# Retrieval scores on one core: one resident chunk fewer, one chunk pair more, biases seeded into PSUM by ScalarE

## What is computed

```python
retrieved = jnp.mean(item_embeddings[indices], axis=1)          # [512, 512]
fused_input = jnp.concatenate([user_rep, retrieved], axis=1)    # [512, 1024]
fused_rep = fused_input @ W_fuse + b_fuse                       # [512, 512]
logits = fused_rep @ W_proj + b_proj                            # [512, 12500]
```

## Time and profile before

| | us |
|---|---|
| runs | 309.22, 310.26, 312.52 |
| median | 310.26 |
| the profiled execution | 309.87 |
| its span, first to last instruction | 308.0 |
| PE busy | 296.9 |
| VectorE busy | 248.3 |
| ScalarE busy | 128.1 |
| POOL busy | 74.9 |

### The profile page before, as it was taken

The page is one execution under the profiler, slowest core; times in us unless marked ns, Lnnn a source line. Parts: engine busy times, 40 slices in busy tenths (PEclk is TensorE's granted clock), DMA queues, the critical chain, the costliest instruction groups (busy, mean ns, idle before and its releaser), DMA issues.

```text
span 308.0 us, 4024 instructions
## 1 busy us (share of the span) xinstructions
PE 296.9 (96%) x1384; PEld 242.3 (79%) x1384; DVE 248.3 (81%) x371; ACT 128.1 (42%) x164; POOL 74.9 (24%) x76
## 2 busy tenths in 40 slices
PE   3999999699999999999999999999999999999995
PEld 1559887498888889888887888888888888888884
DVE  5898998778987836999689989979799797996123
ACT  1104664430010012435375575655846458463310
POOL 4766886787777200000000000000000000000000
PEclk9999999999999999999999999999999999999999
DMA  7999999999996322367538966839677494343315
GB/s 271 337 377 312 358 400 377 409 361 403 291 304 211 107 100 69 130 226 277 198 137 324 318 257 220 313 136 292 240 239 295 146 360 159 135 138 128 131 70 199
DMA packets 32547, 75.13 MB, mean 244 GB/s; under 512 B 4511, under 2 KB 20655, under 8 KB 32528
## 3 DMA queue, kind: packets, MB, share of 16 engines
q1 hardware_dynamic: 25264, 58.06, 52.6%
q0 software_dynamic: 5536, 13.73, 13.6%
q10 hardware_dynamic: 1728, 3.10, 2.6%
HBM read 52.85 MB, written 25.60 MB: 255 GB/s over the span
## 4 chain that ended last, share of the span: by engine, by line
PE 80%; DMA 10%; DVE 6%; issue 1%; ACT 1%; POOL 0%; SPq 0%; POOLq 0%; DVEq 0%; ACTq 0%
PE pair L1137 25%; PE pair L1215 15%; PE pair L1217 15%; PE pair L1218 15%; DMA early<-w_proj 7%; PE pair L1083 4%; PE pair L1123 3%; DMA ring<-item_embeddings,rows 2%; DVE w_lo L833 2%; DVE w_lo L919 1%; DMA early<-w_fuse 1%; DVE pair L796 1%; PE pair L1168 0%; DVE t_sums L908 0%; PE pair L1089 0%
## 5 line engine op out<-in xcount | busy, mean ns | idle before, releaser
L440 POOL DMA_INDIRECT ring<-item_embeddings,rows x56 | 59.8, 1067 | 20.3 <-issue 14.0
L1137 PE MATMUL pair<-w_hi,f_hi 128*128 128x500 f32 x144 | 56.7, 394 | 1.8 <-DVE w_lo L833 1.8
L1137 PE MATMUL pair<-w_lo,f_hi 128*128 128x500 f32 x144 | 56.3, 391 | 0.0
L1137 PE MATMUL pair<-w_hi,f_lo 128*128 128x500 f32 x144 | 56.0, 389 | 0.0
L1215 PE MATMUL pair<-w_hi,s_hi 128*128 128x500 f32 x128 | 49.9, 390 | 0.0
L1217 PE MATMUL pair<-w_lo,s_hi 128*128 128x500 f32 x128 | 49.9, 390 | 0.0
L1218 PE MATMUL pair<-w_hi,s_lo 128*128 128x500 f32 x128 | 49.8, 389 | 0.0
L796 DVE SCALAR_TENSOR_TENSOR pair<-ring,mask,pair 128x512 f32<-128x512 f32 x48 | 36.1, 752 | 3.3 <-DVE pair L810 0.5
L1215 PE MATMUL pair<-w_hi,f_hi 128*128 128x500 f32 x96 | 37.3, 389 | 0.1
L1218 PE MATMUL pair<-w_hi,f_lo 128*128 128x500 f32 x96 | 37.2, 388 | 0.0
L1217 PE MATMUL pair<-w_lo,f_hi 128*128 128x500 f32 x96 | 37.2, 387 | 0.0
(11 more groups left out here) (138 smaller groups left out, 433.2 us busy)
## 6 DMA issues: line engine op xcount, KB each, us to landing
w_raw<-w_proj SPq DMA_DIRECT2D x26, 500.0 KB, 8.1
early<-w_proj SPq DMA_DIRECT2D x24, 500.0 KB, 6.7
logits<-part_out SPq DMA_DIRECT2D x21, 500.0 KB, 3.4
logits<-out_sb SPq DMA_DIRECT2D x28, 250.0 KB, 2.3
logits<-out_sb SPq DMA_DIRECT2D x10, 500.0 KB, 3.0
logits<-out_sb ACTq DMA_DIRECT2D x8, 250.0 KB, 7.0
early<-b_proj SPq DMA_DIRECT2D x8, 250.0 KB, 9.9
s_sum<-b_proj SPq DMA_DIRECT2D x8, 250.0 KB, 6.9
```

Source lines behind the costliest of these rows:

```text
L440: return nc.gpsimd.indirect_dma_start(out=to, out_offset=None, in_=table, in_offset=bass.IndirectOffsetOnAxis(ap=column, axis=0), **how)
L1137: m = nc.tensor.matmul(ps[:, 0:CHUNK], f[:, t, k, :], w, start=begin, stop=(f is f_lo and k == HK - 1))
```

## The change

- `RESIDENT` goes from 8 to 7, `ROUNDS` from 8 to 9. The single chunk 8 and its banks, loads and evacuations are gone.
- ScalarE handles the groups of blocks 1 and 2 and the first three of block 3 (`COPIED = 24` groups with block 0): `seed(t, c)` copies a bias row from SBUF into the bank before PE's first matmul there, the 12 matmuls add onto it, and `copy_out` copies the bank into the output slot. PE waits for `seeded` instead of for an evacuation. Only groups (3, 3) to (3, 6) are still evacuated with an addition by VectorE; their bias rows come in one DMA into `part_out`.
- The bias rows 0 to 3 are loaded after chunk 6 has landed, into the half of `early` that chunk 3 has left, and rows 4 to 6 when chunk 6 is split.
- The list product of tile 1 (`turn_slots`) moves from ahead of the block's last chunk into its middle, next to the turn. VectorE adds tile 1's slots 8 to 10 before it makes `w_lo` of chunk 6's second half, and the home row in the middle of chunk 5.
- The sums for the rounds (`f_total`, `s_start`, `s_next`, `s_end`) are made piece by piece, those of tiles 0 and 1 from the turn of tile 3 on. The blocks of rounds 0 and 1 are loaded between the stores of blocks 1 and 2 and at the start of block 3.
- ScalarE's `keep_sum(0, 1)` stands ahead of the cast of T2 of round 1, and units lie at new places (`unit_place`).

The core of the diff:

```diff
-RESIDENT = 8
-ROUNDS = 8
+RESIDENT = 7
+ROUNDS = 9
-BIAS_SLOTS = 8
+BIAS_AT = (4, 5, 6, 7, 0, 1, 2)
+COPIED = 3 * RESIDENT + 3
...
+            sp.wait_ge(w_landed[raw_of(RESIDENT - 1)][1], 16 * raw_uses(RESIDENT - 1))
+            for c in range(RESIDENT):
+                if BIAS_AT[c] >= HK:
+                    sp.wait_ge(lo_ready, 2 * 4)
+                    load_bias(c)
+            for c in range(RESIDENT):
+                if BIAS_AT[c] < HK:
+                    sp.wait_ge(lo_ready, 2 * RESIDENT)
+                    load_bias(c)
...
+            sp.wait_ge(projected, group_of(TILES - 1, 0) + 1)
+            sp.dma_start(part_out[:, :, :, :].rearrange("p a b n -> p (a b n)").unsqueeze(1),
+                         bp_dram[:, 3 * CHUNK:RESIDENT * CHUNK].unsqueeze(1).to_broadcast([P, 1, 4 * CHUNK]))\
+              .then_inc(late_bias_landed, 16)
...
+            def copy_out(t, c):
+                g = group_of(t, c)
+                act.wait_ge(projected, g + 1)
+                if g >= OUT_SLOTS:
+                    act.wait_ge(out_stored[g % OUT_SLOTS], 16 * (g // OUT_SLOTS))
+                nc.scalar.copy(out_sb[:, g % OUT_SLOTS, :], group_bank(t, c)[:, 0:CHUNK]).then_inc(copied, 1)
...
+            def seed(t, c):
+
+                act.wait_ge(bias_landed[c], 16)
+                if c == 2:
+                    act.wait_ge(ret_ready, HK * (t + 1))
+                else:
+                    act.wait_ge(copied, group_of(t, c - 3) + 1 if c > 2 else group_of(t - 1, RESIDENT - 2 + c) + 1)
+                nc.scalar.copy(group_bank(t, c)[:, 0:CHUNK], bias[:, BIAS_AT[c], 0:CHUNK]).then_inc(seeded, 1)
...
+                if t and g < COPIED:
+                    pe.wait_ge(seeded, g - RESIDENT + 1)
...
             def turn_sum(t):
                 if t == 1:
+                    turn_slots()
                     pe.wait_ge(added, adds_done(1, last_add(1)))
...
-            for t in range(TILES - 1):
-                project(t, RESIDENT, single_ps[t])
```

More of the change, by code:

```diff
@@ L373, in store_pair @@
                   .then_inc(pair_stored[e % OUT_SLOTS], 16)
+            for c in range(RESIDENT):
+                store(1, c)
             for k in range(2):
@@ L625, in seed_c @@
                 else:
-                    act.wait_ge(evacuated, TILES * RESIDENT - RESIDENT + 4)
+                    act.wait_ge(f_ready, HK * TILES)
                 nc.scalar.copy(c_ps[:, :, 0:CHUNK], pair_bias[i % 2][0].unsqueeze(1).to_broadcast([P, 2, CHUNK]))\
                   .then_inc(c_seeded, 1)
+            unit_hi_of(0, B11)
+            copy_out(2, RESIDENT - 2)
+            seed(3, 0)
+            mean(3)
+            copy_out(2, RESIDENT - 1)
+            fused_hi(3, (0, 1))
+            seed(3, 1)
+            fused_hi(3, (2, 3))
+            seed(3, 2)
             s_hi_of(0)
-            split_hi(RESIDENT)
-            unit_hi_of(0, B11)
+            copy_out(3, 0)
             s_hi_of(1)
-            for u in range(T2, UNITS):
+            copy_out(3, 1)
+            unit_hi_of(0, T2)
+            copy_out(3, 2)
+            unit_hi_of(0, B21)
+            unit_hi_of(0, T3)
+            seed_b(0)
+            seed_c(0)
+            for u in (T1, T4, B22):
                 unit_hi_of(0, u)
-            seed_b(0)
+            keep_sum(0, 0)
             unit_hi_of(1, B11)
-            keep_sum(0, 0)
-            seed_c(0)
+            keep_sum(0, 1)
             unit_hi_of(1, T2)
@@ L647, in _ @@
                     keep_sum(i, 0)
-                if not i:
-                    keep_sum(0, 1)
                 if more:
@@ L988, in _ @@
             add(1, 7)
-            split_lo(5)
+            split_lo(5, (0,))
             add_home(1)
-            split_lo(6)
+            split_lo(5, (1,))
+            split_lo(6, (0,))
             for i in range(8, last_add(1) + 1):
                 add(1, i)
-            split_lo(7)
-            for t in range(TILES):
+            split_lo(6, (1,))
+            add_last(2)
+            add_pair(2, 0)
+            add(2, 2)
+            fused_lo(1, (0, 1))
+            add(2, 3)
+            fused_lo(1, (2, 3))
+            add(2, 4)
+            for t in (1, 2):
                 for c in range(RESIDENT):
-                    if t + 1 < TILES and t and c < RESIDENT - 2:
+                    if c < RESIDENT - 1:
                         add(t + 1, AHEAD + 2 * c)
@@ L1031, in _ @@
-                    if t:
-                        evacuate(t, c)
-                    if c == RESIDENT - 1 and t in (1, 2):
-                        fused_lo(t + 1)
-                if t + 2 < TILES:
-                    add(t + 2, 4)
-            unit_lo_of(0, T3)
-            for t in range(TILES):
-                if t == TILES - 1:
-                    t_sum(1, 1)
-                evacuate(t, RESIDENT)
-                if t < 3:
-                    unit_lo_of(0, T1 + t)
+                        if t == 1 and c == 1:
+                            sort(3)
+                    elif t == 1:
+                        add_last(3)
+                        add_pair(3, 0)
+                    else:
+                        unit_lo_of(0, B11)
@@ new lines, in _ @@
+                if t == 1:
+                    fused_lo(2)
+                    add_pair(3, 2)
+                    add(3, 4)
+            f_total(0)
+            fused_lo(3, (0,))
+            s_start(0)
+            fused_lo(3, (1,))
+            s_next(0)
+            fused_lo(3, (2,))
+            s_end(0)
+            fused_lo(3, (3,))
+            t_sum(0, 1)
+            s_lo_of(0)
+            f_total(1)
+            s_start(1)
+            s_next(1)
+            s_end(1)
+            t_sum(0, 2)
```

251 lines of the change are left out of this document (114 added, 137 removed).

## The result

| | before | changed |
|---|---|---|
| median, us (20 runs each) | 310.45 | 311.99 |
| lowest to highest | 309.00 to 312.52 | 310.45 to 314.66 |
| the profiled execution, and its span | 309.87, 308.0 | 314.05, 312.2 |

The ratio is 1.0049, with an interval of 1.0027 to 1.0072. Predicted were 307.0 us and a range of 305.0 to 309.8: the sign is wrong and the time is 5.0 us off.

A forecast was written before the change was run, and what follows sets the result against it. PE's matmul count times pace was taken to bound the kernel from 62 us on. Savings of 3.04 (matmuls), 0.2 (gap) and 0.1 (earlier gathers) made 3.3 us: 307.0 us against the median, range 305.0 to 309.8.

The forecast's parts named there:

- Matmuls: Direct part and rounds: chunks 7 and 8 become a ninth pair, one bias matmul goes; 3.04 us less at unchanged pace.
- Seeds and copies: ScalarE's bias seeds and copies in the direct blocks: a 500-column seed takes 0.57 us, PE never waits on `seeded`; cost 0.
- The first seeds: Before fuse 1: first bias row lands 6.4 us after issue, at 59.8, before ScalarE needs it; nothing waits.
- The gap: End of tile block 0: idle stays about 3 us, now caused by gathers; fuse 1 near 60.9, gain 0.2 us.
- The turns: Turns of tiles 2 and 3: last adds finish 1.0 and 0.9 us ahead of PE; cost 0.
- the rival's wait: Turns of tiles 2 and 3: a turn waits for its gathers, giving 307.9, or 308.8 us for both; chance 0.08.
- 5 us of slack at least; nothing waits: Hand-over to rounds: loads due at 121.6 for the first late evacuation, PE asks at 127.0; no cost.
- the rival of the three output slots: Block 1: copies wait for stores three groups back, drifting from 7.1 us landing; 315.0 us at 12.3 landing; chance 0.05.
- mark of 301.5 for the last matmul: End of the rounds: a sign to check, PE's last matmul near 301.5 us.
- a product of round 0 that waits for its kept sum: Rounds 0 or 1: a product waits for its unit, bias or kept sum; price 1 to 3 us; chance 0.05.
- no clock is to be won: Direct part and rounds: granted clock is already 1.00, so no time was assigned to the clock.
- such waits only take from the one that follows: Chunk 5 of block 0: late `w_lo` loses 0.5 us, which only shortens the next wait; no cost.

The follow-up runs named there:

- E1: Changed kernel with the two block loads of round 1's second half issued behind stores (3,0) and (3,1); 309.48 us, ratio 0.9963 to the kernel before.
- E3: Changed kernel with list product and turn done before PE's wait for `w_lo` in chunk 6 of block 0; 312.34 us, ratio 1.0074 to the kernel before.
- E5: Changed kernel with PE running matmuls nobody reads in its two long waits (9 and 13); 311.25 us, ratio 1.0035 to the kernel before.
- E9: E1 plus the second chunk of round 0's pair loaded behind store (2,5), turn left in place; 308.47 us, ratio 0.9902 to the kernel before.
- E2: Changed kernel with stores (3,0) to (3,2) issued from ScalarE's own queue, SP's loads unchanged; 309.36 us, ratio 0.9963 to the kernel before.
- E11: Changed kernel with VectorE's last sum and rest of B21 of round 0 ahead of evacuating group (3,3); 308.76 us, ratio 0.9935 to the kernel before.
- E4: Changed kernel with the edits of E1 and E3 together; 308.13 us, ratio 0.9923 to the kernel before.
- E6: E1 with tile 1's list product put back ahead of the block's last chunk; 308.11 us, ratio 0.9946 to the kernel before.
- E7: E4 with the second chunk of round 0's pair (1 MB) loaded behind store (2,5) instead of (2,2); 306.24 us, ratio 0.9870 to the kernel before.
- E8: E7 with round 0's first result evacuated ahead of the rests of B21 and T3 of round 1; 306.71 us, ratio 0.9884 to the kernel before.
- E10: The kernel of E7 timed again, unchanged; 306.53 us, ratio 0.9850 to the kernel before.

## Why the prediction was wrong

**Right.** *Matmuls*: 13 fewer, an unchanged pace in the rounds. *Seeds and copies*: PE never waits on `seeded`, and a seed of 500 columns costs what a copy does. The groups of copy and seed, beside the 573 ns of the earlier trace rows:

```profile
L535 ACT COPY out_sb<-pair 128x500 f32<-128x500 f32 x24 | 13.8, 575 | 23.3 <-PE pair L1184 23.3
L549 ACT COPY pair<-early 128x500 f32<-128x500 f32 x17 | 9.9, 581 | 1.6 <-ACT out_sb L535 0.8
```

*The first seeds*: no bias row held one up; the first landed at 60.9 (6.7 us after issue, 6.4 forecast), ahead of its seed at 63.88. In E1's execution, where the whole part is later, it landed at 64.4 and the seed followed at 64.50, so there is little to spare. *The gap* at the end of block 0: VectorE's last `w_lo` released PE at 57.50, the forecast's 57.5. PE had come to the wait 1.0 us later than forecast (55.57 for 54.6), so the wait is 1.93 us and not 2.9. Less the 1.6 us of clock behind it, fuse 1 would have started at 60.7, for 60.9 forecast. *The turns*: none waited, and where an experiment took away the 1 us of slack the rival's wait appeared.

**Wrong: "5 us of slack at least; nothing waits" in the hand-over.** This step failed, in two ways. The slack was worked out for the late bias alone, by its landing at 120.6 (the trace has 114.96 + 7.3 = 122.3). It left out the other thing for which the same evacuation waits, its output slot. The store of (3,0) stands in SP's queue behind 3.5 MB, and landed at 127.6. The mechanism was in the text: the rival of the three output slots has that very cycle, and gives 7.1 us as the landing from which it hurts. But it was placed in block 1 only, with the words that the block loads no longer stand in that window. In block 3 they do. And the slack was counted up to 127.0, when PE asks for that bank. There PE did not wait; VectorE's list was not followed any further, and as it is full from 128 us on it carried the delay to T4, 20 us later. The term put at nothing measured 2.4 us (E3) to 2.65 (E5) on PE.

Another 0.95 us stays after E1. Counted from the kernel before, fuse 3 to the last matmul is 304.35 - 115.64 = 188.7; less 60 direct matmuls (13.65) and plus the ninth pair (19.03) it is 194.1, and E1 has 195.04. The 0.8 us that T4 still waits are most of it. (The forecast's mark of 301.5 for the last matmul is a little later than its own sum, 304.35 - 3.3 = 301.05.)

What came true is one of the three rivals with the least chance (0.05), a product of round 0 that waits for its kept sum, at its upper price of 3 us, though with another reason: the text looked at ScalarE's order, and it was VectorE that came late.

**Wrong: "no clock is to be won".** True of the kernel before, whose 3.2 us of idle time came in pieces of 1.0 us and less. The change gathers the gap into one piece of 1.9 us and adds one of 3.0. The forecast gave such idle time its length as price. The clock cost 1.6 us behind the first and 2.4 to 2.7 behind the second in the profiled execution, and 0.8 (E5) to 1.2 (the changed kernel's own runs) in a mean run.

**Left out: the spread ahead of fuse 1.** Without a fallen clock fuse 1 came at 61.15 in E5, 61.76 in E9 and 62.96 in E1, for 60.9 forecast. In E1 PE also waits 2.1 us in the chunks ahead for `w_lo`; the prediction had said that such waits only take from the one that follows, and in E1 that one is 1.9 all the same.

The sum, for the profiled execution: 306.6 (the forecast on its scale) + 1.4 (fuse 3 at 108.48 for 107.1: the 1.6 of clock, less 0.2) + 5.0 (200.08 - 195.04: the store's wait and the clock behind it) + 0.95 (the rest of the hand-over) = 314.0, and it took 314.05. For the median: 307.0 + 2.4 to 2.65 (store) + 0.95 + 0.8 to 1.2 (clock) = 311.2 to 311.8. The remaining 0.2 to 0.8 to 312.0 lies inside the spread of fuse 3 (107.4 in E5, 109.1 in E1, against 107.1 forecast), which no run here splits up.

## What to carry to other kernels

When loads are moved up in a queue, list what is issued behind them and who waits for that, stores above all: the engine that waits for a store's landing may be one that the change never touched. A slot or bank cycle worked out for one stage has to be tried in every stage that uses the slots. When something comes late to an engine, follow that engine's list until it next has a pause: the wait shows where its delay first reaches the engine that sets the time, here 20 us later. Count an idle stretch of TensorE by its length and its pieces: several short ones were cheaper here than one long one. Moving independent TensorE work (here the turn) ahead of the wait was worth 1.9 us where the next releaser (the gathers) had slack, and nothing in E3, where it had none.

## What the runs showed of the hardware that was not expected

- The granted clock fell to its lower level after a stop of 1.93 us in the changed kernel, 1.92 in E2 and E11 and 1.86 in E4, and did not after 1.90 in E1, 1.94 in E9, and 1.96 and 2.99 in E3's profiled execution. So at these lengths it goes one way or the other. By runs with a mean clock under 0.9965: 28 of 32 with the stop of 3.0 us present (changed kernel, E3), 17 of 34 with one of 1.9 us (E1, E2, E11), but 2 of 18 in E4 and E9, 2 of 12 with one of 1.2 us (E6), 5 of 73 in the kernel before, whose stops are 1.0 us and shorter once the products have begun, and 0 of 29 with all of them short or filled (E5, E7, E8, E10).
- A store of 250 KB took 10.4 us with 3.5 MB issued ahead of it in its queue, 7.9 with 2.5 MB ahead, and 7.6 in another engine's queue with all the loads still in SP's (one execution each). A queue of its own was worth about as much as 1 MB less in front, and its first packet was seen 3 us after the issue.
- Matmuls nobody reads, put into the waits, kept the mean clock above 0.9965 in 12 of 12 runs. The kernel was 0.7 us faster in the median, but with overlapping intervals (ratios 1.0035 and 1.0049), so the gain in time is not clear of noise.
